# A two-layer graph network on one core: half of a norm moved by a step, two reciprocals ahead of a mask, and a Newton step moved from VectorE to GpSimd

## The reference

```python
h = relu(layernorm(x))                              # first norm, over the 512 features
q, k, v = (heads(h @ W + b) for W, b in ...)        # 16 heads of 32
scores = where(adj == 0, -inf, q @ k.T / sqrt(32))
x = x + softmax(scores, -1) @ v -> (h @ Wo + bo)    # layer 1
h = relu(layernorm(x))                              # second norm
alpha = relu((h @ wq) @ (h @ wk).T) * (adj != 0)
alpha = softmax(alpha, axis=1)                      # the second softmax
x = x + alpha @ (h @ weight)                        # layer 2
```

## Time and profile before

| | |
|---|---|
| median of three runs | 1620.14 us (1619.84 to 1623.53) |
| profiled execution | 1615.62 us |
| span of its trace | 1613.8 us |
| granted TensorE clock | 0.996 of full |
| TensorE busy | 1498.3 us, 93% |
| VectorE busy | 1316.8 us, 82% |
| ScalarE busy | 1129.5 us, 70% |
| GpSimd busy | 1018.6 us, 63% |

### The profile page before, as it was taken

The page is one execution under the profiler, slowest core; times in us unless marked ns, Lnnn a source line. Parts: engine busy times, 40 slices in busy tenths (PEclk is TensorE's granted clock), DMA queues, the critical chain, the costliest instruction groups (busy, mean ns, idle before and its releaser), DMA issues.

```text
span 1613.8 us, 50717 instructions
## 1 busy us (share of the span) xinstructions
PE 1498.3 (93%) x16561; PEld 1102.2 (68%) x16561; DVE 1316.8 (82%) x4202; ACT 1129.5 (70%) x2477; POOL 1018.6 (63%) x1286
## 2 busy tenths in 40 slices
PE   2889999999999999999999999999999999999996
PEld 1556777776777767677777677776667777767763
DVE  6788888888888888888888888888888888888773
ACT  3657776777777777777777777777777777777761
POOL 1556667667666766666766766676666676666561
PEclk9999999999999999999999999999999999999998
DMA  8758767666667765766766666676676676676660
GB/s 234 134 105 143 140 129 156 149 141 145 137 130 149 156 148 128 151 139 129 157 149 140 146 137 129 151 156 145 129 151 137 130 158 149 139 147 137 122 123 33
DMA packets 656197, 226.27 MB, mean 140 GB/s; under 512 B 611488, under 2 KB 627872, under 8 KB 656160
## 3 DMA queue, kind: packets, MB, share of 16 engines
q1 hardware_dynamic: 636848, 188.57, 58.1%
q10 hardware_dynamic: 19312, 37.23, 7.9%
HBM read 57.94 MB, written 16.78 MB: 46 GB/s over the span
## 4 chain that ended last, share of the span: by engine, by line
PE 53%; DVE 27%; issue 11%; ACT 4%; POOL 1%; DMA 1%; DVEq 1%; ACTq 0%; POOLq 0%; SPq 0%
PE ring L409 43%; DVE wk_raw L865 9%; PE pv L484 3%; PE score L465 3%; DVE heads_t_lo L959 2%; PE ring L519 2%; DVE newton L908 2%; DVE stage L946 2%; DVE o_sum L880 2%; DVE work L985 1%; DVE l_max L1000 1%; PE pv L486 1%; ACT val L668 1%; DVE e_lo L1016 1%; POOL wv_raw L1124 1%
## 5 line engine op out<-in xcount | busy, mean ns | idle before, releaser
L1124 POOL TENSOR_TENSOR wv_raw<-wk_raw,wv_raw 128x512 f16<-128x512 f32 x512 | 594.2, 1163 | 428.7 <-ACT wv_raw L639 428.5
L626 ACT ACTIVATE wk_raw<-wk_raw,least 128x256 f32<-128x256 f32 x1024 | 458.9, 497 | 8.4 <-DVE least L865 8.3
L865 DVE CUSTOM_DVE_ANT_0 wk_raw<-score,far,undo_score 128x256 f32<-128x256 f32 x1024 | 443.8, 477 | 11.7 <-DVE far L1036 11.4
L639 ACT ACTIVATE wv_raw<-wk_raw 128x512 f16<-128x512 f32 x512 | 320.4, 626 | 9.5 <-issue 4.5
L484 PE MATMUL pv<-val,turned 128*128 128x65 f16 x2048 | 185.8, 192 | 25.5 <-DVE o_sum L880 21.3
L484 PEld LDWEIGHTS pv<-val,turned 128*128 128x128 f16 x2048 | 148.3, 97 | 88.7 <-issue 39.6
L1143 POOL TENSOR_TENSOR heads_out<-o_sum,o_rcp 128x64 f32<-128x64 f32 x512 | 154.4, 323 | 76.2 <-DVE o_sum L880 72.7
L409 PE MATMUL ring<-wv_hi,h 128*128 128x256 f16 x1024 | 188.8, 273 | 1.6 <-DVE wv_lo L828 1.6
L409 PE MATMUL ring<-h,wq_hi 128*128 128x256 f16 x1024 | 175.5, 273 | 7.6 <-DVE wk_lo L828 7.6
L486 PE MATMUL pv<-val,turned 128*128 128x33 f16 x2048 | 177.9, 179 | 0.0
L409 PE MATMUL ring<-h,wk_hi 128*128 128x256 f16 x1024 | 175.1, 273 | 0.0
(11 more groups left out here) (147 smaller groups left out, 3570.9 us busy)
## 6 DMA issues: line engine op xcount, KB each, us to landing
xin<-x_dram ACTq DMA_DIRECT2D x32, 512.0 KB, 3.7
out_dram<-xo SPq DMA_DIRECT2D x32, 512.0 KB, 3.6
xa<-x_dram ACTq DMA_DIRECT2D x31, 512.0 KB, 4.1
adj_in<-adj_dram SPq DMA_DIRECT2D x32, 256.0 KB, 2.8
turned<-wv_raw SPq DMA_TRANSPOSE x512, 3.1
adjt_in<-adj_t_dram SPq DMA_DIRECT2D x32, 256.0 KB, 3.2
wq_raw<-wq_dram SPq DMA_DIRECT2D x2, 512.0 KB, 6.0
wk_raw<-wk_dram SPq DMA_DIRECT2D x2, 512.0 KB, 7.6
```

What stands on the lines that cost most here:

```text
L626: last = nc.scalar.activation(probs[:, at, q, :], probs[:, at, q, :], ACT.Exp, bias=least[:, at, q:q + 1], scale=-1.0)
L639: nc.scalar.activation(halves[:, at, :, 0, :], probs[:, at, :, :], ACT.Copy).then_inc(hi["p"], 1)
L865: last = nc.vector.tensor_tensor_reduce(out=probs[:, at, q, :], in0=score[u % GROUP][:, q * NODES:(q + 1) * NODES], in1=far[:, q, :], scal ...
L1124: nc.gpsimd.tensor_tensor(halves[:, at, :, 1, :], probs[:, at, :, :], halves[:, at, :, 0, :], ALU.subtract).then_inc(lo["p"], 1)
```

## The change

Three edits in the order of the work; what is computed stays. The second half of `first_low` moves from step 1 to step 2, behind that step's low halves. The reciprocals of the second softmax move ahead of the mask of step 12 (they stay behind the copy of `far`). And the first norm's Newton step, three fused instructions and a negation on VectorE, becomes six plain instructions on GpSimd at the head of `first_normalise`; four of them wait for their own semaphore. VectorE's instructions for the second norm's Newton step stay as they are.

```diff
-HIGH1_STEP, LOW1_STEPS, TURN1_STEP = 14, (0, 1), 6
+HIGH1_STEP, LOW1_STEPS, TURN1_STEP = 14, (0, 2), 6
...
-            def reciprocal_deviation(which, b):
+            def reciprocal_deviation(b):
...
-                if which == 0:
-                    nc.vector.tensor_scalar(minus_mean[:], meanvar[0][:, :, 0], -1.0, None,
-                                            ALU.mult).then_inc(negated, 1)
...
+                    if s == AL_STEP + 1 and prev:
+                        second_reciprocal(p)
                     for by in MASKS_AHEAD[s % GROUP][:1 if s == LATE_MASK else 2]:
                         head = ahead(s, by, t, cur, nxt)
                         if head:
                             mask(*head)
                     if s == VAR2 and prev:
-                        reciprocal_deviation(1, p)
+                        reciprocal_deviation(p)
                         second_normalise(p)
-                    if s == NORM1 and later:
-                        reciprocal_deviation(0, n + 1)
                     if s == AL_STEP + 1 and prev:
-                        second_reciprocal(p)
                         second_low(p)
                     if s in STATS1 and later:
                         first_stats(STATS1.index(s), n + 1)
-                    if s in LOW1_STEPS and cur and nxt:
-                        first_low(LOW1_STEPS.index(s), n)
+                    if s == LOW1_STEPS[0] and cur and nxt:
+                        first_low(0, n)
                     for name in DENSE[s]:
...
+                    if s == LOW1_STEPS[1] and cur and nxt:
+                        first_low(1, n)
...
             def first_normalise(b):
-                pool.wait_ge(negated, count(b, 1, 0))
+                y, a, c = rstd[0][:], newton[0][:, 1, :], newton[0][:, 2, :]
+
+                def step(ins, at):
+                    ins.then_inc(nstep[0], 1)
+                    pool.wait_ge(nstep[0], count(b, 2 * NSTEPS, at))
+                    settle(pool, pool_settled)
+
+                pool.wait_ge(rooted[0], count(b, 1, 0))
                 settle(pool, pool_settled)
+                nc.gpsimd.tensor_scalar(minus_mean[:], meanvar[0][:, :, 0], -1.0, None, ALU.mult
+                                        ).then_inc(nstep[0], 1)
+                nc.gpsimd.tensor_scalar(c, meanvar[0][:, :, 1], EPS, -1.0, ALU.add, ALU.mult
+                                        ).then_inc(nstep[0], 1)
+                step(nc.gpsimd.tensor_tensor(a, y, y, ALU.mult), 2)
+                step(nc.gpsimd.tensor_tensor(c, a, c, ALU.mult), 3)
+                step(nc.gpsimd.tensor_scalar(c, c, 1.5 / ROOT, None, ALU.add), 4)
+                step(nc.gpsimd.tensor_tensor(y, c, y, ALU.mult), 5)
                 for q in range(QT):
```

More of the change, by code:

```diff
@@ L263, in two_layers @@
         far_ok = sem("far_ok")
-        const_ok, negated = sem("const_ok"), sem("negated")
+        const_ok = sem("const_ok")
         logged = [sem("logged1"), sem("logged2")]
@@ L897, in first_stats @@
                     aggregate(0, b)
-            def reciprocal_deviation(which, b):
-                y, a, c = rstd[which][:], newton[which][:, 1, :], newton[which][:, 2, :]
+            def reciprocal_deviation(b):
+                y, a, c = rstd[1][:], newton[1][:, 1, :], newton[1][:, 2, :]
                 def step(ins, at):
-                    ins.then_inc(nstep[which], 1)
-                    dve.wait_ge(nstep[which], count(b, NSTEPS, at))
-                dve.wait_ge(rooted[which], count(b, 1, 0))
+                    ins.then_inc(nstep[1], 1)
+                    dve.wait_ge(nstep[1], count(b, NSTEPS, at))
+                dve.wait_ge(rooted[1], count(b, 1, 0))
                 step(nc.vector.scalar_tensor_tensor(out=a, in0=y, scalar=-1.0, in1=y,
                                                     op0=ALU.mult, op1=ALU.mult), 0)
-                step(nc.vector.scalar_tensor_tensor(out=c, in0=meanvar[which][:, :, 1], scalar=EPS,
+                step(nc.vector.scalar_tensor_tensor(out=c, in0=meanvar[1][:, :, 1], scalar=EPS,
                                                     in1=a, op0=ALU.add, op1=ALU.mult), 1)
@@ L1084, in _ @@
                 first_stats(q, 0)
-            reciprocal_deviation(0, 0)
             for q in range(QT):
```

## The result

The changed kernel takes 1571.84 us (median of four runs, 1568.15 to 1573.28) against 1620.68 for the kernel before (1619.84 to 1623.53). The ratio is 0.9697, 95% interval 0.9683 to 0.9711: 48.8 us less, where 40 were forecast and 1580 us stood as the time. The span of its profiled execution is 1566.4 us.

A forecast was written before the change was run, and what follows sets the result against it. TensorE bounds the kernel, except two gaps where VectorE does, together 1.65 us per batch. 0.48 + 1.02 - 0.15 = 1.35 us, times 30 is 40.5, less 0.5 at the start: net 40, giving 1580 us, range 1567 to 1604.

The forecast's parts named there:

- What bounds the kernel: TensorE bounds each batch except at two gaps, 0.58 and 1.07 us, where it waits for VectorE.
- Edit three: First norm's second low half goes behind wo0, so L959 starts earlier and the second gap closes: 1.02 us saved per batch.
- the 0.15 us for the wait at g0: New wait of TensorE at g0's weight load, as the moved half delays wo1's addition; bounds 0 and 0.35.
- Edit two: Second softmax's reciprocals go ahead of the mask, so ScalarE's scaling no longer waits: 0.73 us less, less up to 0.2.
- Edit one: First norm's Newton step goes from VectorE to GpSimd: 1.45 us leave VectorE's queue, ScalarE's exponentials start 0 to 0.5 earlier.
- both edits together put L1016 0.55 to 1.2 us earlier: Newton step and reciprocals together advance VectorE's low half ahead of the pair sum; first gap closes but for 0.1, 0.48 saved.
- the cover is used up when the six take over 5 us: GpSimd's six Newton instructions cost nothing until 5 us, counting the mask that reuses head 14's buffer as first VectorE reader.
- Rival 1: Moved half loses the race with GpSimd for the shared memory path, held up to 1.16 us; about 1611 us, chance 0.12.
- forecast margin of 0.1 us: Lead of the moved half's new start, 683.83, over GpSimd's start on head 6's low half, about 683.93.
- Rival 3: Slower: GpSimd's Newton step is long and delays head 14's low half; at 8.4 us about 1675, chance 0.03.
- Rivals 2 and 4: Second: only one gap goes, about 1592, chance 0.15. Fourth: gaps come back elsewhere, about 1618, chance 0.05.
- 0.15 + 0.05 + 0.1 us a body: Waits left in the forecast: 0.15 new at g0, 0.05 of the second gap, 0.1 of the first.

The follow-up runs named there:

- the run with the memset: The changed kernel with a memset of 256 columns on VectorE just ahead of the moved low half: 1574.6 us, ratio 0.9731.

## Why the prediction was right, and where it was not

**What bounds the kernel** was right. Both gaps belonged to VectorE, nothing else was close, and the 49.1 us by which the two waits shrank are the gain but for the 1.6 lost at the start.

**Edit three** was right in mechanism and close in size: 1.02 us a body forecast, 30.4 / 30 = 1.01 measured alone. Its one wrong term was the 0.15 us for the wait at g0: TensorE's wait there did not grow. Counted from the first product of the output projection, wo1's addition starts 0.38 us later than before (0.35 forecast), the second norm's scaling 0.37, and h2's low half 0.03: short pauses of VectorE between these two took the lateness up.

**Edit two** was right that ScalarE's 0.73 us wait goes and that this closes the gap of 0.58. It was mis-sized in the sum only by the 0.1 left over (0.48 forecast; the gap closed whole, 1590.92 - 1571.84 = 19.1 us or 0.64 a body).

**Edit one** was wrong as a contribution. The step "both edits together put L1016 0.55 to 1.2 us earlier" gives the right number, 1.14 measured, but its reading as a shared gain failed: 0.83 come of edit two alone, which is enough for the gap, and edit one alone gives 0.02. It brings L1003 0.53 us forward (0 to 0.5 forecast for what hangs on it), and then the scaling of the sums is held by GpSimd for nearly as much. I had seen that L1003 was held and did not ask the same of its like further on. The sum did not suffer, because edit two alone suffices; that is luck. At the start edit one costs 1.58 us, three times the 0.5 forecast: the whole delay reaches TensorE's first product, and none of it hides beside the loads. The price of the six GpSimd instructions, 2.2 us, was right to 0.04; "the cover is used up when the six take over 5 us" was not. I took the mask for the first reader, and the transpose for TensorE came first, at 3.7 us.

**Rival 1** was a real mechanism, and the place of the moved half decides: 1571.84 at the end of step 2, 1593.7 at the end of step 1, 1599.13 when made late by a wait. The forecast margin of 0.1 us was right by start times (665.17 against 665.25). The real one is larger by some 0.2 us, as a half that started 0.19 behind GpSimd still went first and one at 0.23 was held. Its price was close, 27 us against 31 forecast, but TensorE waits at the second norm's transposes and not at g0. **Rival 3** has its mechanism too, beyond 3.7 us, and steeper than reckoned because the clock falls. Rivals 2 and 4 did not come.

The forecast was 8 us too high: 0.15 + 0.05 + 0.1 us a body, times 30, is 9, for waits that I left in as residues and that vanished. The start gives 1.1 of it back.

## What to carry to other kernels

Where one engine is nearly full, list its few waits, and price an edit only by the wait that it ends; work taken off another engine is worth nothing where no such wait lies behind it. Moving an instruction to an engine that shares a path to memory with its old one shifts every later instruction of both against each other, so look for the next small instruction that will be held, and do not count on a start that is a hundredth of a microsecond on the good side. Slack has to be read for every reader of a result, the DMA ones too, and the shortest counts.

## What the runs showed of the hardware

- VectorE's scaling of two columns (TENSOR_SCALAR, one input) took 0.16 to 0.17 us in mid-run when it was free and 0.59 to 0.64 when it was held by a GpSimd instruction under way; it then ended 0.03 us behind it. The reciprocal of the same size took 0.17 in every row shown, 0.16 to 0.18 in all traces. The Trainium skill (SBUF — State Buffer, section "Who interferes with whom") names the reason: copies and `tensor_scalar` can run in a mode that uses both ports, and only these, or instructions with two SBUF inputs, contend with GpSimd. The traces agree.
- By the profile's start times GpSimd's claim counts only some 0.2 us behind its start. Over all bodies of the traces, the scaling went ahead of GpSimd's normalisation when it started up to 0.177 us behind it, and was held from 0.175 us on (28 bodies of the changed kernel, at 0.183 to 0.193). The half, against GpSimd's subtraction, went ahead in 29 bodies at 0.18 to 0.19 us (the run with the memset) and was held in mid-run at 0.23 and at 0.31, with and without a wait ahead of it. Why the bound lies where it does isn't shown.
- After 3.26 us in which TensorE waited, its granted clock was at 0.64 over the next 4 us, and 0.963 over the run. Waits of 0.76 us left it at 0.99.
